# The expert groups as a loop on each engine instead of a written-out program

## The reference, cut to what matters

```python
biased = sigmoid(xt @ gate_w.T) + gate_b
_, idx = lax.top_k(biased, TOPK)            # 4 of 16 experts per token, 4096 tokens
w = take_along_axis(scores, idx, axis=-1); w = w / sum(w) * ROUTE_SCALE
for e in range(16):
    y += comb[:, e] * ((silu(xt @ w1[e].T) * (xt @ w3[e].T)) @ w2[e].T)
y += shared expert
```

## Time and profile before

| what | value |
| --- | --- |
| median of 3 runs | 1702.5 us (1701.51 to 1710.38) |
| the profiled execution's own time | 1709.13 us |
| its span, first to last instruction | 1707.5 us, 28004 instructions |
| PE busy | 1155.1 us (68%), 8159 matmuls |
| DVE busy | 1075.5 us (63%) |
| ACT busy | 619.3 us (36%) |
| POOL busy | 522.3 us (31%) |
| mean granted TensorE clock | 0.825 of full speed |
| instruction packets of the whole run | 71 on queue 8 (1.16 MB), 33 on queue 14 (0.27 MB) |
| the groups of expert rows | from 489 us (first matmul) to 801.7 us (end of the last scatter) |

### The profile page before, as it was taken

How to read it: one execution, slowest core, us unless ns; L and a number is a source line. 1 busy time by engine, 2 the same in 40 slices (tenths; PEclk the granted TensorE clock), 3 DMA queues, 4 the chain that set the end, 5 groups by cost and what they waited for, 6 DMA issues and landing times. The chain is left out here.

```text
span 1707.5 us, 28004 instructions
## 1 busy us (share of the span) xinstructions
PE 1155.1 (68%) x8159; PEld 582.6 (34%) x8159; DVE 1075.5 (63%) x2419; ACT 619.3 (36%) x893; POOL 522.3 (31%) x599
## 2 busy tenths in 40 slices
PE   3799954433147777764167648878878788887766
PEld 2455532122024444442033412323323233332455
DVE  4989865543224444442677467878868788885475
ACT  0455542111002111111122304556656566656530
POOL 1333326577625555555110051111111111111110
PEclk7999986566577888886578857989989999999988
DMA  5011002122386656650666631111111211110002
GB/s 185 19 38 37 19 10 73 66 85 92 128 213 143 142 136 140 143 128 15 223 205 222 176 86 35 49 54 34 35 35 38 65 35 34 35 35 2 1 0 98
DMA packets 190082, 141.17 MB, mean 83 GB/s; under 512 B 127240, under 2 KB 162827, under 8 KB 189978
## 3 DMA queue, kind: packets, MB, share of 16 engines
q1 hardware_dynamic: 166058, 84.70, 20.0%
q0 software_dynamic: 18720, 50.70, 8.5%
q10 hardware_dynamic: 5200, 4.33, 0.8%
HBM read 53.56 MB, written 69.01 MB: 72 GB/s over the span
## 5 line engine op out<-in xcount | busy, mean ns | idle before, releaser
L1719 DVE TENSOR_REDUCE small<-ps 128x1 f32<-128x480 f32 (+6 forms) x768 | 419.2, 595 | 106.0 <-PE ps L1771 98.9
L1697 ACT ACTIVATE region<-ps 128x1024 f32<-128x1024 f32 (+5 forms) x384 | 322.8, 880 | 237.6 <-PE ps L1828 236.2
L1669 POOL TENSOR_SCALAR_AFFINE_SELECT region<-region 128x512 f32<-128x512 f32 (+2 forms) x160 | 87.2, 546 | 498.8 <-ACT region L1697 498.8
L866 POOL DMA_INDIRECT token_rows<-region,small x174 | 171.0, 983 | 169.9 <-DVE small L1077 121.2
L1844 PE MATMUL ps<-region 128*32 128x512 f32 (+5 forms) x1792 | 201.4, 510 | 30.2 <-POOL region L1669 20.6
L1771 PE MATMUL ps<-region 48*128 48x480 f16 (+6 forms) x896 | 159.6, 345 | 46.0 <-DVE small L1719 45.5
L1202 PE MATMUL ps<-region 128*128 128x384 f16 x696 | 152.3, 380 | 41.7 <-DMA region<-expert_rows 41.6
L858 POOL DMA_INDIRECT expert_rows<-region,small x128 | 128.7, 1006 | 44.6 <-issue 37.5
L1828 PE MATMUL ps<-region 50*128 50x512 f16 (+5 forms) x896 | 133.9, 335 | 12.4 <-issue 10.2
L1213 PE MATMUL ps<-region 128*128 x522 | 82.4, 314 | 84.4 <-DVE region L1092 83.1
L1766 PE MATMUL ps<-small 64*128 64x128 bf16 (+1 forms) x768 | 91.9, 250 | 38.5 <-DMA region<-v_parts 19.2
(11 more groups left out here) (243 smaller groups left out, 1723.9 us busy)
## 6 DMA issues: line engine op xcount, KB each, us to landing
region<-token_rows POOLq DMA_DIRECT2D x8, 2048.0 KB, 9.9
v_parts<-region SPq DMA_DIRECT2D x16, 576.0 KB, 5.8
region<-v_parts SPq DMA_DIRECT2D x16, 576.0 KB, 4.0
expert_rows<-region SPq DMA_DIRECT2D x17, 391.5 KB, 2.6
region<-k_parts SPq DMA_DIRECT2D x96, 68.0 KB, 2.2
region<-q_parts SPq DMA_DIRECT2D x96, 64.0 KB, 2.1
k_parts<-region SPq DMA_DIRECT2D x16, 272.0 KB, 3.7
x_sb<-in_x ACTq DMA_DIRECT2D x8, 512.0 KB, 9.5
```

Of the source, the lines that this page charges most:

```text
L866: nc.gpsimd.indirect_dma_start(out=ys, out_offset=bass.IndirectOffsetOnAxis(ap=home[:, g % HOMES, j:j + 1], axis=0), in_=y_out[:, b, j, :] ...
L1669: nc.gpsimd.affine_select(out=t, in_=t, compare_op=ALU.is_ge, fill=0.0, base=r0, pattern=[[0, G], [1, w]], channel_multiplier=-1).then_inc ...
L1697: nc.scalar.activation(dst, src, ACT.Exp, scale=SCALE).then_inc(s_exp, 1)
L1719: nc.vector.tensor_reduce(nmp[:, qt, half, p0:p0 + np_, place], bank[:, 0:np_ * nk].rearrange("p (h k) -> p h k", h=np_), AX.X, ALU.max).t ...
```

## The change

The 58 groups are no longer written out. Each engine gets a loop of seven turns with eight groups in its body (LOOP = HOMES = 8), and two groups behind it; DVE has its first turn written out ahead of the loop, since that turn has fewer waits. All buffer numbers stay constants of the body, because eight is a multiple of all depths. What depends on the group becomes a register: the place in the tables of experts and first rows, and the count of nearly every wait. The waits of SP, POOL, DVE and PE become hold; ACT's stay plain waits with a register. Waits that the first groups didn't have are now there for all, and five one-element fills on DVE give their semaphores a credit at the start. PE loads the expert's number twice for a group, once for gate_up and once for down, since it can't be carried from turn to turn.

```diff
+            LOOP = HOMES
+            PER = LOOP // G_BUFS
+            LOOPS = (GROUPS - 2) // LOOP
+            assert Y_BUFS == G_BUFS == 4 and LOOPS * LOOP + 2 == GROUPS
+            def group_loop(eng, body, peeled=0):
+                for i in range(peeled):
+                    for b in range(LOOP):
+                        body(i, b, True, True)
+                with eng.Fori(peeled, LOOPS) as i:
+                    for b in range(LOOP):
+                        body(i, b, True, True)
+                body(LOOPS, 0, True, False)
+                body(LOOPS, 1, False, False)
...
-                for g in range(GROUPS):
-                    b = g % G_BUFS
-                    if g >= G_BUFS:
-                        sp.wait_ge(s_ggu, g - G_BUFS + 1)
-                        sp.wait_ge(s_home, g - G_BUFS + 1)
-                    first = sp.value_load(start_tab[0:1, g:g + 1], min_val=0, max_val=E * STRIDE)
-                    sp.dma_start_transpose(xgT[:, b].rearrange("p s k n -> p (s k) n"),
-                                           xs[bass.ds(first, GROUP), 0:D].bitcast(F16)).then_inc(s_xg[b], 16)
-                    sp.dma_start(tags[:, b], xs[bass.ds(first, GROUP), D:ROW].rearrange("(j p) n -> p j n", p=P)
-                                 ).then_inc(s_xg[b], 16)
+                def read_group(i, b):
+                    g = i * LOOP + b
+                    hold(sp, s_ggu, g + 1, s_tick)
+                    hold(sp, s_home, g + 1, s_tick)
+                    first = sp.value_load(start_tab[0:1, bass.ds(g, 1)], min_val=0, max_val=E * STRIDE)
+                    sp.dma_start_transpose(xgT[:, b % G_BUFS].rearrange("p s k n -> p (s k) n"),
+                                           xs[bass.ds(first, GROUP), 0:D].bitcast(F16)).then_inc(s_xg[b % G_BUFS], 16)
+                    sp.dma_start(tags[:, b % G_BUFS], xs[bass.ds(first, GROUP), D:ROW].rearrange("(j p) n -> p j n", p=P)
+                                 ).then_inc(s_xg[b % G_BUFS], 16)
+                with sp.Fori(0, LOOPS) as i:
+                    for b in range(LOOP):
+                        read_group(i, b)
+                for b in range(GROUPS - LOOPS * LOOP):
+                    read_group(LOOPS, b)
...
+                def send_back(i, b, more, ahead):
+                    g = i * LOOP + b
+                    hold(pool, s_home, g + G_BUFS + 1, s_tick)
+                    hold(pool, s_yout, g + 2, s_tick)
                     for j in range(GT):
                         nc.gpsimd.indirect_dma_start(
-                            out=ys, out_offset=bass.IndirectOffsetOnAxis(ap=home[:, g % HOMES, j:j + 1], axis=0),
-                            in_=y_out[:, b, j, :], in_offset=None, bounds_check=B * L * TOPK - 1,
-                            oob_is_err=False).then_inc(s_back[b], 16)
+                            out=ys, out_offset=bass.IndirectOffsetOnAxis(ap=home[:, b, j:j + 1], axis=0),
+                            in_=y_out[:, b % Y_BUFS, j, :], in_offset=None, bounds_check=B * L * TOPK - 1,
+                            oob_is_err=False).then_inc(s_back[b % Y_BUFS], 16)
+                group_loop(pool, send_back)
...
+                def group_silu(i, b):
+                    i, b = at_group(i, b)
+                    g, v = i * LOOP + b, b % 2
+                    act.wait_ge(s_ggu, g + G_BUFS + 1)
+                    act.wait_ge(s_gh, g + 1)
+                    nc.scalar.activation(sg_buf[:, v, :], ps[:, 2 + 2 * v, 0:GROUP], ACT.Silu,
                                          scale=1.0 / WS).then_inc(s_gsilu, 1)
-                    act.wait_ge(s_gh, g + 1)
-                    if g >= 2:
-                        act.wait_ge(s_gy, g - 1)
-                    nc.scalar.activation(hgh[:, g % 2, :], hg_buf[:, g % 2, :], ACT.Copy).then_inc(s_ghh, 1)
-
-                for g in range(GROUPS):
-                    silu(g)
+                    act.wait_ge(s_gh, g + 2 + 1)
+                    act.wait_ge(s_gy, g + 1)
+                    nc.scalar.activation(hgh[:, v, :], hg_buf[:, v, :], ACT.Copy).then_inc(s_ghh, 1)
+                def body(i, b, more, ahead):
+                    if more:
+                        group_silu(i, b + 1)
+                group_silu(0, 0)
+                group_loop(act, body)
...
+                for at_, (signal, n) in enumerate(((s_ggu, G_BUFS), (s_home, G_BUFS), (s_gh, 2), (s_gy, 2), (s_yout, 1))):
+                    credit(nc.vector.memset(top[:, 0, at_:at_ + 1], 0.0), signal, n)
...
+                def homes(i, b):
+                    i, b = at_group(i, b)
+                    g, v = i * LOOP + b, b % 2
                     order = Order(dve, s_hself, 2 * g)
-                    dve.wait_ge(s_xg[b], (g // G_BUFS + 1) * 32)
-                    order.mark(nc.vector.scalar_tensor_tensor(out=which[:, v], in0=tags[:, b, :, 0:TOPK], scalar=expert_of[:, g:g + 1],
-                                                              in1=by_r[:], op0=ALU.is_equal, op1=ALU.mult))
+                    hold(dve, s_xg[b % G_BUFS], turn(i, b) * 32 + 32, s_tick)
...
+                    if not isinstance(i, int) or i:
+                        hold(dve, s_back[b % Y_BUFS], (turn(i, b) - PER + 1) * GT * 16, s_tick)
...
+                def group_hidden(i, b):
+                    i, b = at_group(i, b)
+                    g, v = i * LOOP + b, b % 2
+                    hold(dve, s_gsilu, g + 1, s_tick)
...
+                    hold(dve, s_ghh, g + 1, s_tick)
...
+                def group_out(i, b):
+                    g = i * LOOP + b
+                    hold(dve, s_gy, g + 2 + 1, s_tick)
+                    if not isinstance(i, int) or g >= Y_BUFS:
+                        hold(dve, s_back[b % Y_BUFS], turn(i, b) * GT * 16, s_tick)
...
+                homes(0, 0)
+                homes(0, 1)
+                group_hidden(0, 0)
+                group_loop(dve, body, 1)
...
+                def expert(i, b):
+                    return pe.value_load(expert_tab[0:1, bass.ds(i * LOOP + b, 1)], min_val=1, max_val=E)
+                def group_gate_up(i, b):
+                    e = expert(i, b)
+                    i, b = at_group(i, b)
+                    g, v = i * LOOP + b, b % 2
+                    hold(pe, s_xg[b % G_BUFS], turn(i, b) * 32 + 32, s_tick)
+                    hold(pe, s_gh, g + 1, s_tick)
...
+                def group_down(i, b):
+                    e = expert(i, b)
+                    g, v = i * LOOP + b, b % 2
+                    hold(pe, s_ghl, g + 1, s_tick)
+                    hold(pe, s_yout, g + 1, s_tick)
...
+                def body(i, b, more, ahead):
+                    if more:
+                        group_gate_up(i, b + 1)
+                    group_down(i, b)
+                group_gate_up(0, 0)
+                group_loop(pe, body)
```

More of the change, by code:

```diff
@@ L801, in flat, with turn, at_group @@
                 return t.rearrange("p a n -> p (a n)")
-            def returned(g):
-                return (g // Y_BUFS + 1) * GT * 16
+            LOOP = HOMES
[11 more added lines that the diff above has]
+                body(LOOPS, 1, False, False)
+            def turn(i, b):
+                return i * PER + b // G_BUFS
+            def at_group(i, b):
+                return i + b // LOOP, b % LOOP
             @block.sync
@@ L1088, in group_out @@
[L1088 to L1091, removed]
-                    nc.vector.tensor_copy(y_out[:, g % Y_BUFS].rearrange("p j d -> p (j d)"),
-                                          ps[:, 6:8, :].rearrange("p a n -> p (a n)")[:, 0:GT * D]).then_inc(s_yout, 1)
-                homes(0)
-                homes(1)
-                group_hidden(0)
-                for g in range(GROUPS):
-                    if g + 2 < GROUPS:
-                        homes(g + 2)
-                    if g + 1 < GROUPS:
-                        group_hidden(g + 1)
-                    group_out(g)
+                    if not isinstance(i, int) or i:
+                        hold(dve, s_back[b % Y_BUFS], (turn(i, b) - PER + 1) * GT * 16, s_tick)
@@ new lines, in group_out @@
+                def group_out(i, b):
[3 more added lines that the diff above has]
+                        hold(dve, s_back[b % Y_BUFS], turn(i, b) * GT * 16, s_tick)
+                    nc.vector.tensor_copy(y_out[:, b % Y_BUFS].rearrange("p j d -> p (j d)"),
+                                          ps[:, 6:8, :].rearrange("p a n -> p (a n)")[:, 0:GT * D]).then_inc(s_yout, 1)
+                def body(i, b, more, ahead):
+                    if ahead:
+                        homes(i, b + 2)
+                    if more:
+                        group_hidden(i, b + 1)
+                    group_out(i, b)
@@ L1201, in group_gate_up @@
                                 w = flat((w13h, w13l)[low][:, bass.ds(e, 1), kh * D + half_ * P:kh * D + half_ * P + P])
-                                ins = nc.tensor.matmul(ps[:, 2 + 2 * (g % 2) + half_, 0:GROUP], w, xgT[:, g % G_BUFS, part, kh, :],
```

(25 more changed lines are left out.)

33 lines of the change are left out of this document (8 added, 25 removed).

## The result

On one chip the changed kernel took 1722.29 us (median of 9 runs, 1717.3 to 1727.9), the kernel before 1707.81 us (9 runs, 1694.21 to 1710.86): a ratio of 1.0093, 95% interval 1.0068 to 1.0118 (the two medians alone give 1.0085). The forecast was 1704 us against 1702.5, no change; the measured time lies inside the range, and rival A had given 1722. The profiled execution took 1721.55 us, its span was 1719.8 us.

What follows compares the result with a forecast made beforehand. Late signals at an unnamed fixed rate, probably DMA traffic, were taken to bound the groups. Start 0.5 + end 0.9 + nothing for 28 pairs = 1.4 us: 1709.13 to 1710.5, less 6.6 to the runs' median, 1704 us; range 1690 to 1730.

Steps and rivals of the forecast that it cites:

- rival A: Pairs of groups: added PE and DVE steps carry into each of 28 pairs, 18 us, 1722 us; chance 0.20.
- I take nothing: Pairs of groups: of a possible 0 to 0.64 us more for each of 28 pairs, the forecast counted none.
- 2.9 us of slower matmuls: Two pairs before the change: PE's matmuls ran 2.9 us longer at clock 0.68 than at 0.99, the pair no longer.
- The 0.64 us: Estimated added sequencer steps on the chain of a pair of groups, PE and DVE together.
- DVE's 0.26: DVE between the down product's signal and its copy: two waits, a count and three gaps, 0.26 us.
- PE's 0.38: PE between a down and the gate behind it: two counts, one wait and one place, 0.38 us.
- 0.5 us at most, beside 2.4 us free: New steps on POOL, SP and ACT: 0.5 us a group at most, beside 2.4 us free on POOL.
- The 8.5 us at the start: First groups: silu waits 8.5 us for "remote" at 512.22, read as a fixed rate whose store fills once.
- The DMA traffic: Groups' stage: inferred source of the fixed rate behind the late signals, some 3 us of waiting per two groups.
- the branch: PE's loop: 0.22 us for each of six branches back, covered, so nothing added; upper end 3.53 us six times.
- rival C: Groups' stage: more idle time keeps PE at the low clock, 99 us, 1803 us at its end; chance 0.04.
- The start: Stage's start: five one-element fills on DVE lie on its path, 0.5 us (0.2 to 0.8).

## Why the forecast of no change failed, and what of it held

**The step that failed** is "I take nothing" for the steps of a pair. Its reason was "What 2.9 us of slower matmuls didn't move, 0.64 us of sequencing shouldn't". The earlier trace rows show that the pair doesn't follow PE, and that was right: more matmuls, an earlier down and moved steps of PE made no difference to the time that stands clear of noise. But it doesn't follow that the pair follows nobody. The 0.64 us were 0.38 on PE and 0.26 on DVE, and the argument held for the first alone. The measured term is 0.63 us a pair, as large as the estimate, but that is luck, since it is made of other parts. DVE's 0.26 is there, as estimated: the copy starts 0.25 us behind the signal instead of 0.02. A part of 0.18 us was in no estimate: the low halves run later on DVE, meet the second scatter, and the burst takes 7.58 us instead of 7.40. The rest, some 0.2 us of the mean pair, isn't placed. Taking back DVE's holds and loop gave 0.7 of the 0.93%. PE's 0.38 shows on PE itself in the pairs at the full clock, but moving it away brought no gain that can be told, and what PE, ACT and SP cost together lies between nothing and 0.5% and stays open. So rival A was right that steps add up, but the runs show it only of those on DVE.

**The cover.** POOL was put aside with "0.5 us at most, beside 2.4 us free". The free time was no cover, though not for the steps that I had in mind (POOL's own were harmless). Of the 4.7 us that POOL has free in a pair (10.58 - 5.88), 1.5 us are five gaps of 0.3 us between one scatter and the next, and 3.2 us are the way round from the burst's end to the next burst. A busy share counts neither. The row that should have told is in the earlier trace rows: POOL's 5.88 us and six instructions, equal in three pairs in which everything of PE differs.

**The 8.5 us at the start**, read as "a store ahead of it that fills once": the first burst has nine scatters, whose last one starts at 509.37; the silu at 512.22 comes 1.9 us behind its end. That is the pattern of the circle, only with a longer burst; no run tested it.

```profile
509.37 0.98 POOL L866 DMA_INDIRECT token_rows<-region,small  x1 [0.30 <-issue]
```

**The DMA traffic**, to which I gave the rate by inference: in part. Plain row loads took 0.8% off, but the late signals stayed.

**Right** were the branch (0.22 taken, 0.21 measured) and the clock (0.84 in the stage against 0.82, rival C out). The start (0.2 to 0.8 us) can't be judged: the first matmul came 1.9 us later, and the execution's own spread is in it. Under rival C, the 3.79 us "after the gap" were not the first work behind it. The down from 610.17 to 611.32 was granted 1.00 of the full clock, and the gate from 611.32 on 0.54.

**Open**: why two signals of PE, those of the last down and gate in a burst, come only 1.1 to 1.6 us (medians) behind the end of POOL's last scatter, while an earlier one passes at once: in the kernel before the silu at 615.03 stands in the midst of the burst of 610.78 to 618.18, 0.04 us behind the recorded end of gate and up (611.20 + 3.79). Whether it is the issue on POOL or the landing of the data was not separated.

## What to carry to other kernels

If the length of a repeating pattern doesn't change with one engine's work, look for the column that is equal in all its turns before putting the rate outside the engines; a busy share leaves out the gaps between back to back DMA issues and the way round to the next burst, so a queue that is busy for 54% of the time, as POOL's was, can be the bound. In a circle, count the new sequencer steps between the signal that comes last and the instruction that starts the next link (here 0.09 to 0.11 us for a held wait), and look whether moved instructions now run beside others that they slow. The other engines' steps count for little until a run says otherwise. Where a copy that feeds several DMAs lies on the circle, splitting it at the DMA's size is worth a try (here 0.65%). The loop with the split copy was not run.

## What the runs showed of the hardware

**Scatters and DVE.** In the changed kernel a scatter that starts while DVE subtracts the low halves (both inputs in SBUF) lasts 1.14 us in the mean (37 of them, 32 over 1.05), and 0.98 when it starts within the multiply, one of whose inputs is in PSUM (36, none over 1.05). In the kernel before 11 started within the subtraction, 3 of them over 1.05. The Trainium skill, "SBUF — State Buffer", section "Who interferes with whom", says that VectorE with two SBUF inputs and a GpSimd operation that reads SBUF contend for a port that they share. The traces agree in which operation collides; the delay of the scatter at 615.97, 0.18 us, is less than the 0.31 us for which the subtraction still ran. The same section also holds that such a two-input operation was not seen to stall the DMAs that GpSimd issues; here it does lengthen their issue, and the measurement decides.

**Branches.** A PE loop with 168 matmuls and 168 weight loads in its turn branches in 0.21 us, and 3 + 3 packets bring instructions in the whole stage. In "Runtime: NRT & Kernel Launch", section "Instruction fetch mechanics", of the Trainium skill the rule of two pages (512 instructions) would have this body of some 544 (the trace records 519 a turn, matmuls, weight loads and sequencer steps together) fetch at each turn, and PE's room for 2048 would not; the trace agrees with the second. Of the loop that pays 3.5 us the trace of before records 2038 such instructions a turn, just under that room, so it neither confirms nor denies it.
